# Moving the second attention's first steps within the last units of a routed product, and cutting one tile from each part's last unit

## What is computed

```
# layer 2: routed feed-forward, one of 8 experts for each row
top_id = argmax(x @ gate_w);  score = sigmoid(max(x @ gate_w))
xs = x * score
act = silu(xs @ rt_gate[e]) * (xs @ rt_up[e])        # 128 -> 256, for each expert e
y = act @ rt_down[e]                                 # 256 -> 128
x = x + shared(x) + y[top_id]
# layer 3: cross attention onto 120 context rows
q, k, v = layernorm(x) @ Wq + bq, ctx @ Wk + bk, ctx @ Wv + bv
x = x + softmax(q k^T / sqrt(128)) v
# layer 4: 8 binary trees of depth 7: logits, a masked silu, an output product
x = x + (silu(logits) * path_mask(logits)) @ W_out.T
```

## Time and profile before

| | us |
|---|---|
| median of 3 runs | 847.22 |
| lowest and highest run | 845.65, 848.89 |
| the profiled execution's own time | 849.45 |
| its span in the trace | 847.6 |
| share of the span in which PE is busy | 93% |
| DVE, ACT, POOL busy | 77%, 64%, 31% |

### The profile page before, as it was taken

How to read it: one execution, slowest core, us unless ns; L and a number is a source line. 1 busy time by engine, 2 the same in 40 slices (tenths; PEclk the granted TensorE clock), 3 DMA queues, 4 the chain that set the end, 5 groups by cost and what they waited for, 6 DMA issues and landing times.

```text
span 847.6 us, 15269 instructions
## 1 busy us (share of the span) xinstructions
PE 787.2 (93%) x4452; PEld 633.5 (75%) x4493; DVE 655.7 (77%) x1742; ACT 541.6 (64%) x948; POOL 265.4 (31%) x308
## 2 busy tenths in 40 slices
PE   5899998987878998999999999999999999999997
PEld 4788776776768898977777777777777777777775
DVE  5888889787844456768988887888888788888774
ACT  3577667565322334366877777777777777778765
POOL 2333222887287143112320321232132133111000
PEclk9999999999999999999999999999999999999999
DMA  6346784742334343100000000000000000000000
GB/s 170 89 137 191 194 221 130 202 130 85 87 108 149 95 116 91 51 26 13 26 23 4 25 25 0 25 25 19 6 25 25 0 25 25 11 14 14 14 1 25
DMA packets 91428, 55.88 MB, mean 66 GB/s; under 512 B 13439, under 2 KB 88055, under 8 KB 91255
## 3 DMA queue, kind: packets, MB, share of 16 engines
q1 hardware_dynamic: 75440, 41.29, 17.4%
q0 software_dynamic: 4096, 8.40, 3.5%
q10 hardware_dynamic: 11847, 5.64, 2.4%
HBM read 32.23 MB, written 23.07 MB: 65 GB/s over the span
## 4 chain that ended last, share of the span: by engine, by line
PE 41%; DVE 28%; issue 12%; ACT 12%; POOL 3%; another core or an unknown queue 2%; DVEq 1%; DMA 0%; ACTq 0%; POOLq 0%; SPq 0%
PE PS L823 7%; PE PS L808 6%; DVE sil_l L1522 4%; DVE dec L1506 3%; DVE xn_c L1149 3%; PE PS L1009 3%; PE PS L1068 3%; PE PS L1069 3%; PE PS L1070 3%; ACT sil L765 3%; DVE xn L1149 2%; PE PS L1090 2%; PE PS L1092 2%; PE PS L1091 2%; DVE st L1138 2%
## 5 line engine op out<-in xcount | busy, mean ns | idle before, releaser
L765 ACT ACTIVATE sil<-PS,b_in_c 128x512 f32<-128x512 f32 x256 | 162.3, 686 | 113.6 <-PE PS L1077 71.3
L1522 DVE TENSOR_TENSOR sil_l<-sil,sil_h 128x512 fp32r<-128x512 f32 x256 | 164.8, 685 | 44.7 <-ACT sil_h L773 44.3
L526 POOL TENSOR_TENSOR ve<-mv,eps 128x4 f32<-128x4 f32 x64 | 19.2, 300 | 450.2 <-DVE mv L1143 450.1
L773 ACT ACTIVATE sil_h<-sil 128x512 fp32r<-128x512 f32 x224 | 128.9, 631 | 0.0
L1090 PE MATMUL PS<-sil_h,wout_l 128*128 128x512 f32 x256 | 117.8, 460 | 1.6 <-DVE sil_l L1522 1.6
L1506 DVE TENSOR_SCALAR dec<-PS,b_in_c 128x512 bf16<-128x512 f32 x128 | 95.6, 747 | 26.1 <-PE PS L1070 24.3
L1068 PE MATMUL PS<-x4T_h,win_l 128*128 128x512 f32 x256 | 102.2, 399 | 1.6 <-ACT yo L725 0.7
L1092 PE MATMUL PS<-sil_h,wout_h 128*128 128x512 f32 x256 | 100.8, 394 | 0.0
L1091 PE MATMUL PS<-sil_l,wout_h 128*128 128x512 f32 x256 | 100.3, 392 | 0.0
L1069 PE MATMUL PS<-x4T_l,win_h 128*128 128x512 f32 x256 | 100.0, 390 | 0.0
L1070 PE MATMUL PS<-x4T_h,win_h 128*128 128x512 f32 x256 | 99.8, 390 | 0.0
(11 more groups left out here) (169 smaller groups left out, 1549.6 us busy)
## 6 DMA issues: line engine op xcount, KB each, us to landing
x_sorted<-zeros SPq DMA_DIRECT2D x4, 1280.0 KB, 6.8
xs_in<-x_sorted SPq DMA_DIRECT2D x20, 256.0 KB
y_sorted<-yo ACTq DMA_DIRECT2D x20, 256.0 KB
X<-in_x SPq DMA_DIRECT2D x16, 256.0 KB
rows<-xn SPq DMA_DIRECT2D x16, 256.0 KB
out<-res SPq DMA_DIRECT2D x16, 256.0 KB
ctxT<-in_ctx_t SPq DMA_DIRECT2D x16, 240.0 KB
ctx_rows<-in_ctx_kv SPq DMA_DIRECT2D x16, 240.0 KB
```

Source lines behind the costliest of these rows:

```text
L765: act.activation(tile(sil[p % 2], c, W), bank(2 * (p % 2) + c), ACT.Silu, bias=b_in_c[:, 2 * p + c:2 * p + c + 1]).then_inc(t_silu, 1)
L773: act.activation(tile(sil_h[p % 2], c, W), tile(sil[p % 2], c, W), ACT.Copy).then_inc(t_hi, 1)
L1522: dve.tensor_tensor(tile(sil_l[p % 2], c, W), tile(sil[p % 2], c, W), tile(sil_h[p % 2], c, W).bitcast(F32), ALU.subtract).then_inc(t_lo, 1)
```

## The change

The change has two parts.

First, each part's last unit, 9 and 19, has three tiles instead of four: a part's rows can fill at most 39 of its 40 tiles, because eight partly filled last tiles cannot add up to more than seven beyond the 32 full ones. `pair_tiles` gives 1 for pair 1 of these two units, where r is a Python number. In unit 9 the weights, silu, multiply, down product, copy and store lose a tile; its gate and up products are issued from the loop, where r is no Python number, and keep theirs. In unit 19 the gate and up products lose it too. The loop on DVE ends two units earlier, so that unit 9 is unrolled there.

Second, early steps stand elsewhere: on DVE `c_norm3(0)` now stands between `r_first(14)` and `r_second(14)`, `c_max_scores(0)` after `r_second(15)`, `c_rows4(0)` after `r_second(17)`, `c_norm4(0)` between the halves of 18 ahead of `c_rows3(1)`, and `c_x4_low(0)` after both multiplies of unit 19. On ACT `c_softmax(0)` and `c_pT_evac(0)` stand ahead of the second silu of bodies 16 and 17, instead of after bodies 15 and 16; `c_x4_high(0)` goes from the end of body 18 to the end of body 19, and `c_xnT_evac(1)` after the last store. On PE `c_turn_prob(0)` goes from inside body 16 to its end, `c_values(0)` from the end of body 16 into body 17, `c_turn_x4(0)` from body 18 into body 19, and `c_turn_x(1)` from body 19 to after the last down product.

```diff
+        def pair_tiles(r, v):
+            return 1 if v and isinstance(r, int) and r in (HR - 1, NR - 1) else 2
...
@@ ACT, r_body @@
-                r_silu(2 * r, 0)
+                r_silu(r, 0)
                 if not last_unit(r):
                     r_evac_x(r + 1, 1 - u)
-                if isinstance(r, int) and r == FIRST_EARLY + 3:
-                    c_xnT_evac(0)
-                r_silu(2 * r + 1, 1)
+                if isinstance(r, int):
+                    if r == FIRST_EARLY + 3:
+                        c_xnT_evac(0)
+                    if r == FIRST_EARLY + 4:
+                        c_softmax(0)
+                    if r == FIRST_EARLY + 5:
+                        c_pT_evac(0)
+                r_silu(r, 1)
...
@@ ACT, behind each unrolled body @@
-                if r == FIRST_EARLY + 3:
-                    c_softmax(0)
-                if r == FIRST_EARLY + 4:
-                    c_pT_evac(0)
-                if r == FIRST_EARLY + 6:
+                if r == FIRST_EARLY + 7:
                     c_x4_high(0)
-                if r == FIRST_EARLY + 7:
-                    c_xnT_evac(1)
             r_evac_y(NR - 1, 1, NR // 2 - 1, 1)
+            c_xnT_evac(1)
...
@@ PE, r_body @@
-                    if r == FIRST_EARLY + 4:
-                        c_turn_prob(0)
-                    if r == FIRST_EARLY + 6:
+                    if r == FIRST_EARLY + 5:
+                        c_values(0)
+                    if r == FIRST_EARLY + 7:
                         c_turn_x4(0)
-                    if r == FIRST_EARLY + 7:
-                        c_turn_x(1)
...
@@ DVE, unrolled bodies @@
-            with dve.Fori(1, HR) as r:
+            with dve.Fori(1, HR - 2) as r:
...
-                if r == FIRST_EARLY + 3:
-                    c_max_scores(0)
-                if r == FIRST_EARLY + 5:
-                    c_rows4(0)
+                if r == FIRST_EARLY + 2:
+                    c_norm3(0)
                 if r == FIRST_EARLY + 6:
+                    c_norm4(0)
                     c_rows3(1)
                 r_second(r, coming)
```

More of the change, by code:

```diff
@@ L85, in program @@
     x_sorted = [nc.dram_tensor(f"x_sorted{h}", (HTILES[h] * P, P), F32, kind="Internal").ap() for h in range(HALVES)]
-    y_sorted = [nc.dram_tensor(f"y_sorted{h}", (HTILES[h] * P, P), F32, kind="Internal").ap() for h in range(HALVES)]
+    y_sorted = [nc.dram_tensor(f"y_sorted{h}", ((HTILES[h] - 1) * P, P), F32, kind="Internal").ap() for h in range(HALVES)]
     rows2 = nc.dram_tensor("rows2", (B, P, P), F32, kind="Internal").ap()
@@ L714, in c_x4_high, with r_silu @@
                 act.activation(x4T_h, bank(7), ACT.Copy).then_inc(c_x4h, 1)
-            def r_silu(q, v):
-                act.wait_ge(r_gu_ps, q + 1)
-                pair = by_tile(PS[:, 512 * (1 + 2 * v):512 * (3 + 2 * v)], 512)
-                act.activation(by_tile(sg[v], FI), pair[:, :, 0:FI], ACT.Silu).then_inc(r_sg, 1)
+            def r_silu(r, v):
+                n = pair_tiles(r, v)
+                act.wait_ge(r_gu_ps, 2 * r + v + 1)
+                pair = by_tile(PS[:, 512 * (1 + 2 * v):512 * (1 + 2 * v + n)], 512)
+                act.activation(by_tile(sg[v][:, 0:n * FI], FI), pair[:, :, 0:FI], ACT.Silu).then_inc(r_sg, 1)
             def r_evac_y(r, u, stores, h):
@@ L820, in r_gate_up @@
                     pe.wait_ge(r_act, q - 1)
-                for t in range(2):
+                for t in range(pair_tiles(r, v)):
                     for n in range(2 * FC):
@@ L1002, in _, with r_down @@
             pe.wait_ge(a_rows, 16 * NG)
-            def r_down(q, v, experts):
-                pe.wait_ge(r_act, q + 1)
-                for t in range(2):
+            def r_down(r, v, experts):
+                pe.wait_ge(r_act, 2 * r + v + 1)
+                for t in range(pair_tiles(r, v)):
                     for c in range(FC):
@@ L1020, in r_body @@
                 if not first(r):
-                    r_down(q - 1, 1, was)
+                    r_down(r - 1, 1, was)
                 if not end:
@@ L1054, in _ @@
                 if r == FIRST_EARLY + 4:
-                    c_values(0)
+                    c_turn_prob(0)
             now = r_body(NR - 1, 1, now, coming, end=True)
-            r_down(2 * NR - 1, 1, now)
+            r_down(NR - 1, 1, now)
+            c_turn_x(1)
             def t_logits(g, p):
@@ L1202, in take_logits, with r_weights @@
                 dve.tensor_tensor(dst, dst, src[:, :, 0:n, E:2 * E], ALU.add).then_inc(a_lg, 1)
-            def r_weights(q, v, experts):
-                if not below(q, 2):
-                    dve.wait_ge(r_gu_ps, q - 1)
-                for t in range(2):
+            def r_weights(r, v, experts):
+                if not below(r, 1):
+                    dve.wait_ge(r_gu_ps, 2 * r + v - 1)
+                for t in range(pair_tiles(r, v)):
                     i = dve.tensor_copy(tile(w_now[v], t, 2 * FI),
@@ L1241, in a_body @@
                     a_choose(4)
-                    r_weights(1, 1, experts_of(dve, 0))
+                    r_weights(0, 1, experts_of(dve, 0))
                 if route == "pack":
@@ L1434, in c_x4_low, with r_mul @@
                 dve.tensor_tensor(x4T_l, bank(7), x4T_h.bitcast(F32), ALU.subtract).then_inc(c_x4l, 1)
-            def r_mul(q, v):
-                dve.wait_ge(r_sg, q + 1)
-                if not below(q, 2):
-                    dve.wait_ge(r_y_ps, q - 1)
-                pair = by_tile(PS[:, 512 * (1 + 2 * v):512 * (3 + 2 * v)], 512)
-                dve.tensor_tensor(by_tile(ract[v], FI), by_tile(sg[v], FI), pair[:, :, FI:], ALU.mult).then_inc(r_act, 1)
+            def r_mul(r, v):
+                n = pair_tiles(r, v)
+                dve.wait_ge(r_sg, 2 * r + v + 1)
+                if not below(r, 1):
+                    dve.wait_ge(r_y_ps, 2 * r + v - 1)
+                pair = by_tile(PS[:, 512 * (1 + 2 * v):512 * (1 + 2 * v + n)], 512)
+                dve.tensor_tensor(by_tile(ract[v][:, 0:n * FI], FI), by_tile(sg[v][:, 0:n * FI], FI), pair[:, :, FI:],
+                                  ALU.mult).then_inc(r_act, 1)
             def c_rows3(h):
@@ L1469, in _ @@
             dve.wait_ge(routed, 2)
-            with dve.Fori(1, HR) as r:
+            with dve.Fori(1, HR - 2) as r:
                 coming = r_first(r)
                 r_second(r, coming)
-            for r in range(HR, NR - 1):
+            for r in range(HR - 2, NR - 1):
                 coming = r_first(r)
@@ L1492, in _ @@
                 if r == FIRST_EARLY + 5:
-                    c_norm4(0)
+                    c_rows4(0)
                 if r == FIRST_EARLY + 6:
-                    c_x4_low(0)
                     c_norm3(1)
-            r_mul(2 * NR - 2, 0)
-            r_mul(2 * NR - 1, 1)
+            r_mul(NR - 1, 0)
+            r_mul(NR - 1, 1)
+            c_x4_low(0)
             def t_decide(g, p):
```

27 lines of the change are left out of this document (15 added, 12 removed).

## The result

| | before | changed |
|---|---|---|
| median, us | 847.67 (9 runs, 845.65 to 849.17) | 851.51 (9 runs, 850.11 to 855.85) |
| ratio of the two, 95% interval | | 1.0049 (1.0033 to 1.0064) |
| the profiled execution's own time | 849.45 | 850.79 |
| its span | 847.6 | 849.0 |

The changed kernel is 3.8 us slower, and the forecast was 1.6. The time of before is now the median of nine runs.

What follows compares the result with a forecast made beforehand. PE was taken as the bound, with only the start of the first tree logits able to move. The forecast was 847.2 - 0.1 (moves and tiles) + 1.7 (one clock fall) = 848.8 us, range 845.5 to 852.1.

Steps and rivals of the forecast that it cites:

- Bound: From 380 to 840 us PE is busy 453.0 of 460.0 us; only that stretch's beginning, set by the first logits, can move.
- Body 15: The maximum and shift leave the space ahead of pair 1's multiply; nothing waits: 6.75 us, against 10.33 before.
- The four waits: PE waits 2.42 us in body 16, 0.74 and 1.58 in body 18, 2.04 in unit 19, giving back body 15's gain.
- The second table load: On ACT in body 16, the silu starts 1.30 us after the load behind the exponential, without the skill page's added drain.
- The tiles: Unit 19's third tile saves about 1.7 us; unit 9 saves nothing, 0.5 us at most.
- The loop's exit: DVE's loop ending two units earlier: taken as zero, bounded by 2.60 us; as a rival 2.6 us on top, 851.4, chance 0.02.
- Bodies 13 and 14: They keep their length, since the moved `c_norm3(0)` (1.02 us) fits inside the 1.6 us DVE has in body 14.
- The clock: Three waits (2.42, 1.58, 2.04 us) at one fall in three: one fall of PE's clock likeliest, costing 1.7 us, chance 0.46.
- The sum: Body 15 to first logits: 6.75 + 8.72 + 6.75 + 12.95 = 35.17 us against 35.23, 0.1 us faster at full clock.
- The waits do not hold PE: Faster rival: early steps find ACT and DVE free, the four waits vanish, 6.8 us go: 840.3 us, chance 0.04.
- the long table switch: Rival: ACT's table switches in body 16 last longer than their loads, 2.8 us on top: 851.6 us, chance 0.01.
- no fall, one and two: Cases by number of clock falls behind the waits: none 847.1 us (0.29), one 848.8 (0.46), two 850.5 (0.13).

Runs made afterwards that it cites:

- tiles_only: Changed kernel with every early step back at its place of before; three-tile units and shorter DVE loop stay: 839.31 us, ratio 0.9989 to before.
- filled kernels: Changed kernel and kernel before, with products nobody reads put on PE in place of waits: 853.32 us (ratio 1.0021) and 852.54 us (1.0000).
- body18: Changed kernel with `c_rows3(1)` in body 15, `c_norm4(0)` behind the second half of body 18, POOL's two deviations in that order: 839.99 us, ratio 0.9998 to before.
- after_again: The changed kernel unaltered, measured again on the second experiment chip against the kernel before: 842.00 us, ratio 1.0018.
- after_beside: The changed kernel unaltered, measured again on the third chip beside the kernels with filled waits: 855.44 us, ratio 1.0032 to before.
- spread: Changed kernel with the same steps reordered to leave none of the four waits (exponential behind `yo`, statistics split off, normalisations later): 835.08 us, ratio 0.9927 to before.
- loop_only: Kernel before with only DVE's loop ended two units earlier, nothing moved and no tile cut: 840.20 us, ratio 0.9997 to before.

## Why the prediction was right, and where it was not

**Bound.** Right. The last stretch kept its length, and the difference lies ahead of the logits.

**Body 15.** Right to the hundredth: 6.75 us, and no wait.

**The four waits.** Forecast 2.42, 0.74, 1.58 and 2.04 us; measured 2.40, 0.82, 1.23 and 2.05, each released by the instruction that was named (`yo`, and three times a multiply). A row counts from the end of the last record, though, and the working from where the next instruction could have started, some 0.16 us earlier. Counted that way the four are 2.56, 0.99, 1.39 and 2.21, 0.4 more together than worked out. That is nearly all of the 0.43 by which the stretch is longer than the sum (35.60 for 35.17). Of the second wait's 0.25, 0.23 come from DVE: the weights began 3.21 us after the addition (351.95 to 355.16), and the sum had 2.98. The third alone is shorter: its gate-up starts at T+6.45 where T+6.39 was written, but PE came to it later, held by the second wait.

**The second table load.** 1.30 us from the load to the silu's start (341.82 to 343.12), as in the earlier trace rows. The drain that the Trainium skill adds to each switch (ScalarE: Activation LUTs, What ACT_TABLE_LOAD costs) would, by an estimate from the figure of that page, have made the wait 2.76 us longer; the trace does not agree.

**The tiles.** Right in kind: 1.4 us in the trace of `tiles_only`, where 1.7 was written. Unit 9 gave nothing, as said. Timeline of PE of the changed kernel, at the turn of unit 11:

```profile
301.33 0.61 PE L1019 MATMUL PS<-WD,ract 128*128 x4
302.18 2.05 PE L833 MATMUL PS<-xsT,w_now 128*128 128x128 f32 x16 [0.24 <-ACT xsT L637]
```

The down product has 4 records instead of 8, and PE then waits for `xsT`.

**The loop's exit.** Zero, as taken: 0.9997.

**Bodies 13 and 14.** They took 13.44 us in the changed kernel and 12.99 before, and a wait of 0.55 us for a multiply stands in body 13, ahead of the moved `c_norm3(0)`. In the eight traces of the first two experiment chips the pair takes 12.14 or 12.15 us in each kernel, with `c_norm3(0)` moved or not, and 12.99 to 13.58 in those of the third. It goes by the chip, not by the change; the statement that they keep their length stands. The sign named for the loop's exit, bodies 8 to 14 longer than 5.9 us, was badly chosen, since the kernel before has 6.01, 6.70 and 6.29 us in bodies 8, 13 and 14.

**The clock.** The forecast said one fall, at 1.7 us. The waits can now be counted over all traces of kernels that have them, without those of the filled kernels:

| wait | traces | falls behind it |
|---|---|---|
| 1.90, body 15, steps as before | 3 | 3 |
| 2.40, body 16 | 5 | 2 |
| 2.11, body 16 of `body18` | 1 | 0 |
| 1.23 to 1.56, body 18 | 6 | 0 |
| 2.05 to 2.15, unit 19 | 6 | 3 |

Where no fall is counted, the granted clock is 1.00 all the way to the next wait of the table, or to some 6 us behind the first logits. That makes 2/5 + 0 + 3/6, about 0.9 falls in one execution of the changed kernel, which is the one that was forecast; the three traces of it have none, two and one. In body 16 a fall costs 1.4 to 1.6 us (the stretches of `after_again`, less its second fall, and of `after_beside`). In unit 19 of `after_again` it costs 0.3 ahead of the logits (2.50 instead of 2.18 from the down product on) and 1.0 behind them (the first twelve tree products take 3.81 us instead of 2.85), 1.3 in all. So falls are worth 0.4 times 1.5 and 0.5 times 1.3, 1.25 us and not 1.7. The rate "one in three" came from three waits of one trace, and is too low for the long waits and too high for the one of body 18; the two errors cancel, which is luck. The same trace had two more long waits ahead of the routed product that the prediction left out, 2.54 us at 146.85 and 3.20 us at 207.66, and the clock fell behind both (the granted clock is 0.50 from 146.85 to 149.00, and 0.57 from 207.66 to 211.65). With them it was three falls in five. The rates are counts of a few traces, and the length of a wait alone does not decide: a fall follows one of 1.39 us in the last section.

**The sum as it now stands**: 35.60 and 1.25 are 36.85 us, against 35.0 before (35.23 and 34.81): 1.8 us slower, where the forecast said 1.6. The three comparisons measured 3.8, 1.5 and 3.0 us. 1.8 lies in the intervals of the second (0.3 to 2.8) and the third (0.3 to 5.1) and below that of the first (2.8 to 5.4). **The other 2 us of the first comparison are not settled.** Two of its nine single times of the changed kernel are 855.5 and 855.9 us at a mean granted clock of 0.981 and 0.985, the others 850.1 to 852.4 at 0.986 to 0.990, which would fit more falls; no trace was taken of those two. And units 3 to 7, which the change leaves alone, differ by 3.3 us between the two traces of this comparison (last section). So the range held with 0.6 us to spare (851.51, its end at 852.1), and only because it had 1.6 us of scatter on top of two falls: the sum that the traces bear out gives about half of what the first comparison measured.

**The rivals.** "The waits do not hold PE" falls by the first timeline. It said that without the four waits 6.8 us would go, and `spread` is 6.9 us under the changed kernel. That the two are so near is partly chance: the 6.9 hold falls of the clock, which the 6.8 do not, and two small waits are left in `spread`. The loop's exit falls by `loop_only`, the long table switch by ACT's timeline. Which of no fall, one and two holds is not one answer but changes from execution to execution.

## What to carry to other kernels

Work that is taken from ahead of one engine's next operation must go to a place where nothing is queued behind it that another engine needs before that engine has something else to do; read for each new place what stands next in the queue and when it is wanted, as the four waits here could be read in advance. In this pipelined body that place was behind the last operation for which PE waits (`yo` on ACT, the second multiply on DVE), and the better places were worth 7 of 840 us with the same work. Do not take the rate of something irregular, such as clock falls, from one trace: take the traces of several kernels that share the wait.

## What the runs showed that was not expected

**One wait, two outcomes.** All 14 traces have a wait of 1.8 to 2.5 us for the second gate-up near 238 us, in a unit that no version changes. In five of them the product behind it takes 2.05 us; in the nine others it takes 2.60 to 3.64. Timelines of PE of `loop_only` and of `tiles_only`, which ran on one chip:

```profile
236.96 2.05 PE L823 MATMUL PS<-xsT,w_now 128*128 128x128 f32 x16 [2.49 <-DVE ract L1442]
```

```profile
237.97 3.64 PE L834 MATMUL PS<-xsT,w_now 128*128 128x128 f32 x16 [2.49 <-DVE ract L1454]
```

The wait is the same to the hundredth, 2.49 us, and the product differs by 1.59. The earlier trace rows show one of the five, from which the prediction took that such a wait brings no fall.

**Executions differ by 4 us before the routed product begins.** On the first two experiment chips its first turn stands between 218.80 and 222.58 us, in kernels that are alike up to there. Part of it is again falls of the clock, in the shared part of layer 2. `loop_only` (first turn at 219.41) and `after_again` (222.53) are still within 0.06 us of each other at 195.9 us. These are rows of PE's timeline of `loop_only`, and then the same products in `after_again`:

```profile
198.90 1.06 PE L831 MATMUL PS<-SD,s_act 128*128 128x128 f32 x8
...
217.53 2.05 PE L831 MATMUL PS<-SD,s_act 128*128 128x128 f32 x16 [0.41 <-DVE s_act L1293]
```

```profile
199.08 1.92 PE L841 MATMUL PS<-SD,s_act 128*128 128x128 f32 x8
...
219.10 3.63 PE L841 MATMUL PS<-SD,s_act 128*128 128x128 f32 x16 [0.76 <-DVE s_act L1302]
```

In `after_again` the granted clock is 0.72 from 197 to 203 us and 0.53 from 219.10 to 222.53; in `loop_only` it is 1.00 in both places. The turn ahead of the first product had waited 1.40 us in `loop_only` and 1.39 in `after_again`. The profiled execution of the changed kernel has both of these falls, that of before only the second. Between the two places lies a wait of about 3 us (2.93 in both of these traces), behind which the clock falls in all 14 traces, at once or about 2 us later. From the product behind it to the next kind of product it is 4.04 us in `loop_only` and 3.82 in `after_again`, so this fall is no part of the difference.

The single times of the kernel before lie in two groups on these chips, 837.8 to 838.5 us and 839.6 to 841.7, with nothing between.

**Units 3 to 7 depend on the chip and the execution.** From the turn of unit 3 to that of unit 8 the eight traces of the first two experiment chips take 30.6 to 30.9 us, the other six 36.8 to 42.8, before and changed kernels alike: 40.14 in the trace of before (241.95 to 282.09), 36.82 in that of the changed kernel. These are the two traces of the first comparison. Bodies 9 to 12 take 5.85 or 5.86 us each in all 14. These rows of PE's timeline are the turns of units 3 and 8 in the changed kernel, and then in `after_again`, which is the same program:

```profile
246.10 0.60 PE L818 MATMUL PS<-WA,xs_in 128*128 128x128 f32 x4
...
282.92 0.65 PE L818 MATMUL PS<-WA,xs_in 128*128 128x128 f32 x4 [0.24 <-issue]
```

```profile
245.01 0.60 PE L818 MATMUL PS<-WA,xs_in 128*128 128x128 f32 x4
...
275.60 0.65 PE L818 MATMUL PS<-WA,xs_in 128*128 128x128 f32 x4
```

These 6 to 12 us are most of why one chip gives 840 us for the kernel before and another 848 or 852. What holds these units is not settled.
